# One layer on one core: the first tile's load shared by two queues, and the early order of ScalarE and VectorE changed

## What is computed

```
def step(carry, kv_t):                      # over the 128 tokens of a sequence
    p, q, o = carry
    no = max(o, u + kt); A = exp(o - no); E = exp(u + kt - no)
    y = (A * p + E * vt) / (A * q + E)
    no2 = max(w + o, kt); A2 = exp(w + o - no2); E2 = exp(kt - no2)
    return (A2 * p + E2 * vt, A2 * q + E2, no2), y

x = x + wkv(w, u, layernorm(x), ctx)
xf = layernorm(x)
gates = softmax(xf @ gate_w + gate_b); combine = the two largest, others 0
routed = sum over e of combine[:, e] * (gelu(xf @ ew1[e] + eb1[e]) @ ew2[e] + eb2[e])
shared = sum over s of gelu(xf @ sw1[s] + sb1[s]) @ sw2[s] + sb2[s]
x = x + shared + routed
```

## Time and profile before

| | us |
|---|---|
| median of three executions | 859.07 |
| lowest and highest of them | 858.18, 859.83 |
| the profiled execution | 859.92 |
| span of its instructions | 858.2 |
| TensorE busy in it | 835.7 |
| VectorE, ScalarE, GpSimd busy | 617.8, 467.1, 237.2 |

### The profile page before, as it was taken

The page is one execution under the profiler, slowest core; times in us unless marked ns, Lnnn a source line. Parts: engine busy times, 40 slices in busy tenths (PEclk is TensorE's granted clock), DMA queues, the critical chain, the costliest instruction groups (busy, mean ns, idle before and its releaser), DMA issues.

```text
span 858.2 us, 14380 instructions
## 1 busy us (share of the span) xinstructions
PE 835.7 (97%) x4102; PEld 692.2 (81%) x4102; DVE 617.8 (72%) x1244; ACT 467.1 (54%) x824; POOL 237.2 (28%) x277
## 2 busy tenths in 40 slices
PE   3899999999999999999999999999999999999998
PEld 2768888888888888878888888888888889998886
DVE  7987889976887778757787787576787544443694
ACT  6577776444466663534656464345555355656442
POOL 4110000233200000225000003232342488854870
PEclk9999999999999999999999999999999999999999
DMA  8913644389533333787433325867798388868987
GB/s 242 297 37 111 173 122 122 110 179 182 121 109 88 100 97 108 175 195 162 102 117 98 99 75 162 156 123 220 210 241 215 117 265 269 270 213 274 308 235 223
DMA packets 130144, 144.24 MB, mean 168 GB/s; under 512 B 11010, under 2 KB 89402, under 8 KB 129568
## 3 DMA queue, kind: packets, MB, share of 16 engines
q1 hardware_dynamic: 117792, 108.88, 48.3%
q0 software_dynamic: 11344, 33.50, 13.2%
q10 hardware_dynamic: 944, 1.07, 0.4%
HBM read 120.43 MB, written 22.98 MB: 167 GB/s over the span
## 4 chain that ended last, share of the span: by engine, by line
PE 89%; DMA 2%; SPq 1%; DVE 1%; issue 1%; ACT 0%; DVEq 0%; ACTq 0%
PE up L640 13%; PE up L642 12%; PE up L641 12%; PE acc L701 12%; PE acc L703 12%; PE acc L707 12%; PE up L885 5%; DMA w_raw<-in_L_ffn_sw 2%; PE acc L640 1%; PE acc L642 1%; PE acc L641 1%; PE misc L666 1%; PE up L666 1%; PE acc L811 1%; PE up L803 1%
## 5 line engine op out<-in xcount | busy, mean ns | idle before, releaser
L640 PE MATMUL up<-xs,w1hi 128*128 128x512 f32 (+1 forms) x512 | 198.4, 387 | 0.1
L642 PE MATMUL up<-xs,w1lo 128*128 128x512 f32 (+1 forms) x512 | 195.5, 382 | 0.0
L641 PE MATMUL up<-xs,w1hi 128*128 128x512 f32 (+1 forms) x512 | 195.4, 382 | 0.0
L963 ACT ACTIVATE hhi<-up,b_col 128x512 fp32r<-128x512 f32 x128 | 86.6, 676 | 199.2 <-PE up L642 161.1
L701 PE MATMUL acc<-w2hi,hhi 128*128 128x512 f32 x486 | 189.7, 390 | 0.0
L703 PE MATMUL acc<-w2lo,hhi 128*128 128x512 f32 x486 | 189.3, 389 | 0.0
L1239 DVE TENSOR_TENSOR hlo<-hf,hhi 128x512 fp32r<-128x512 f32 x128 | 85.6, 669 | 68.7 <-ACT hhi L963 28.6
L707 PE MATMUL acc<-w2hi,hlo 128*128 128x512 f32 x486 | 130.7, 389 | 0.0
L640 PEld LDWEIGHTS up<-xs,w1hi 128*128 128x128 f32 x512 | 96.2, 188 | 18.9 <-issue 0.7
L642 PEld LDWEIGHTS up<-xs,w1lo 128*128 128x128 f32 x512 | 96.2, 188 | 18.7
L641 PEld LDWEIGHTS up<-xs,w1hi 128*128 128x128 f32 x512 | 96.3, 188 | 17.9
(11 more groups left out here) (270 smaller groups left out, 1124.1 us busy)
## 6 DMA issues: line engine op xcount, KB each, us to landing
w_raw<-in_L_ffn_sw SPq DMA_DIRECT2D x256, 256.0 KB, 3.1
expert_rows<-ysb SPq DMA_DIRECT2D x47, 256.0 KB, 3.8
xn_rows<-kn POOLq DMA_DIRECT2D x16, 256.0 KB, 8.5
e2raw<-in_L_ffn_ew SPq DMA_DIRECT2D x16, 256.0 KB, 6.6
ew_sb<-in_L_ffn_ew SPq DMA_DIRECT2D x16, 256.0 KB, 6.8
X<-in_x SPq DMA_DIRECT2D x12, 256.0 KB, 8.6
vin<-in_ctx SPq DMA_DIRECT2D x12, 256.0 KB, 11.6
out<-X SPq DMA_DIRECT2D x12, 256.0 KB, 4.4
```

The costliest lines, as they stand in the source:

```text
L640: nc.tensor.matmul(o, lhs[0], rhs[0], start=start, stop=False)
L641: nc.tensor.matmul(o, lhs[0], rhs[1], start=False, stop=False)
L642: return nc.tensor.matmul(o, lhs[1], rhs[0], start=False, stop=stop)
L963: nc.scalar.activation(hhi[:, slot, tok], up[slot][:, tok], ACT.Gelu, bias=bias).then_inc(h_hi, 1)
```

## The change

Tile 0's four parts are issued two by SP and two by ScalarE's queue, the latter ahead of the vectors. VectorE normalizes tile 0 (`early_ln1_apply(0)`) ahead of `tables`. ScalarE makes `grow`, then tile 0's exponential, then `keep`, then copies tile 0's values, and then makes `boost`. VectorE does `ev` right after the first scan, ahead of `h`, for all four tiles (for tiles 2 and 3 behind `early_ln2_apply`); `ev` waits for the values itself, as `hv` did and does. The names of the counting semaphores follow the new order.

```diff
--- before.py
+++ after.py
@@ -340,11 +340,11 @@
         early2 = Steps(sem("early2"), "s a veps")
         tab = Steps(sem("tab"), "wu neg pos down uw cap")
         boost_arg = sem("boost_arg")
-        tabs0 = Steps(sem("tabs0"), "keep grow boost")
+        tabs0 = Steps(sem("tabs0"), "grow keep boost")
         rec0 = Steps(sem("rec0"), "ln rec")
         tabs = Steps(sem("tabs"), "grow relu boost keep")
         wt = Steps(sem("wt"), "tk tv")
-        wkv0 = Steps(sem("wkv0"), "es cq sq h hv den ev cp sp num nt nr y")
+        wkv0 = Steps(sem("wkv0"), "es cq sq ev h hv den cp sp num nt nr y")
         wkv = Steps(sem("wkv"), "es h ev hv cq sq den cp sp num nt nr y ty")
         wexp = Steps(sem("wexp"), "e ln rec")
         ln2 = Steps(sem("ln2"), "s0 s1 s2 s3 a0 a1 a2 a3 veps")
@@ -528,7 +528,8 @@
                              sw1_c[p // CPS, p % CPS]).then_inc(pw1_in[p], 16)
                 sp.dma_start(early_w2(p), sw2_c[p // CPS, p % CPS]).then_inc(pw2_in[p], 16)
 
-            load_tiles([0])
+            for g in (0, 1):
+                sp.dma_start(X2[32 * g:32 * g + 32, 0, 0], xq[0, g, :, 0]).then_inc(x_tile[0], 16)
             load_tiles([1])
             load_tiles([2, 3])
             load_values([2, 3])
@@ -1057,6 +1058,8 @@
                 nc.scalar.copy(e2hi[:, e], e2raw[:, e]).then_inc(r2hi, 1)
 
             nc.scalar.preload_act_table_set("natural_log_exp_and_others")
+            for g in (2, 3):
+                act.dma_start(X2[32 * g:32 * g + 32, 0, 0], xq[0, g, :, 0]).then_inc(x_tile[0], 16)
             for at, vector in ((0, decay), (CW, bonus)):
                 act.dma_start(wu[at + CB:at + CW], vector.rearrange("(b g p) -> b g p", g=GB, p=32)).then_inc(uw_in, 16)
                 act.dma_start(wu[at:at + CB], vector.rearrange("(b o p) -> b o p", o=1, p=32)
@@ -1083,11 +1086,11 @@
                 nc.scalar.activation(hf[:, n % RING, piece(n)], up[n % RING][:, up_piece(n)], ACT.Gelu,
                                      bias=b1_col[:, p:p + 1]).then_inc(pre_h, 1)
 
-            first_keep()
             first_grow()
             early_exp(0)
+            first_keep()
+            early_values(0)
             first_boost()
-            early_values(0)
             early_values(1)
             for b in range(CB // 2 - 1):
                 table_grow(b)
@@ -1361,6 +1364,7 @@
                                            in1=state(qq)[:, :, 0:TT], op0=ALU.min, op1=ALU.add))
 
             def early_ev(i):
+                dve.wait_ge(v_ok, i + 1)
                 edo(V.tensor_tensor(state(ev)[:, :, 1:], state(es)[:, :, 1:], values(i), ALU.mult))
 
             def early_num(i):
@@ -1642,15 +1646,15 @@
                 const(V.tensor_tensor(bias_s[:], bias_s[:], bias_g[:, 0], ALU.add))
 
             early_ln1(0)
+            early_ln1_apply(0)
             tables()
-            early_ln1_apply(0)
             early_ln1(1)
             early_es(0)
             early_scan(0)
+            early_ev(0)
             early_h(0)
             early_hv(0)
             early_den(0)
-            early_ev(0)
             early_num(0)
             early_result(0)
             early_ln1_apply(1)
@@ -1663,11 +1667,11 @@
             early_ln1_apply(2)
             early_es(1)
             early_scan(1)
+            early_ev(1)
             early_h(1)
             early_hv(1)
             early_den(1)
             early_ln1(3)
-            early_ev(1)
             early_num(1)
             early_ln1_apply(3)
             early_result(1)
@@ -1676,10 +1680,10 @@
             early_ln2(1)
             early_scan(2)
             early_ln2_apply(1)
+            early_ev(2)
             early_h(2)
             early_hv(2)
             early_den(2)
-            early_ev(2)
             early_num(2)
             early_result(2)
             early_es(3)
@@ -1687,10 +1691,10 @@
             early_ln2(2)
             early_scan(3)
             early_ln2_apply(2)
+            early_ev(3)
             early_h(3)
             early_hv(3)
             early_den(3)
-            early_ev(3)
             early_num(3)
             early_result(3)
             x_lo(2, 1, 2, x_bank[2])
```

## The result

The median of twenty executions is 861.5 us (860.51 to 867.91) against 859.3 us (858.18 to 862.82) for the kernel before in as many: a ratio of 1.0029, 95% interval 1.0015 to 1.0042. (The ratios in this document come from all executions of both kernels; they are not the quotients of the medians.) The change makes the kernel slower by 2.2 us. Forecast were 859.9 us, a range up to 861.2 and 0.14 for slower by over 0.2%.

A forecast was written before the change was run, and what follows sets the result against it. The start of TensorE's dense matmuls was taken to bound the kernel, with VectorE setting it. VectorE's path +0.06 and ScalarE's reciprocal path +0.8, the later counting, turned median 859.07 into 859.9 us, range 858.5 to 861.2.

The forecast's parts named there:

- slower by over 0.2%: Rival at TensorE's wait for tile 1's `vin`: parts land ever later, price 1.75 us, 860.8 and above; chance 0.14.
- What bounds the kernel: TensorE's dense matmuls, busy all 186.00 us from 64 to 250, carry any shift of their start to the end.
- First tile on two queues: Tile 0's load: statistics start at about 3.45 us, `kn` at 5.36, 0.83 earlier, keys' transposes done at 7.07.
- What ScalarE's queue pays: Two added parts free ScalarE's queue 0.75 to 0.95 us later; 0.8 taken, so at 7.31.
- Orders, tables and `ev`: ScalarE and VectorE lists: tables and `ev` order cost nothing; `es` starts at 9.23 us, 0.27 later.
- the sum: Tile 0's product: VectorE's path +0.06 us, ScalarE's path to the reciprocal +0.8; the later one counts.
- Values of tile 1: `vin` on ScalarE's queue: landing time kept at 4.9 us, so values shift by their issue, 0.8.
- The upper bound: Landing of tile 1's values: if the quarters' trend continues, 1.84 per microsecond of later issue, 0.95 gives 1.75 us.
- The page's figure: DMA landing of 64 KB estimated at 2.15 us; tile 1's values not late, sum +0.06 in place of +0.8.

The follow-up runs named there:

- e7: Kernel before, with tile 1's values issued by SP behind tile 1's rows and their copy behind the reciprocal; 859.35 us against 860.51, ratio 0.9991.
- e4: Changed kernel, with ScalarE's copy of tile 1's values moved behind tile 0's reciprocal; 861.69 us against 860.75, ratio 1.0010.
- e1: Changed kernel without its queue part: tile 0's four parts all on SP again, new orders kept; 863.64 us against 860.75, ratio 1.0030.
- e8: Kernel before, with two small constants (16 and 8 KB) at the head of ScalarE's queue, tile 0 all on SP; single execution 860.65 us beside 859.82.
- e8b: The same kernel as e8 run once more; single execution 860.09 us beside 859.82 for the kernel before.
- e5: Kernel before, with ScalarE's copy of tile 1's values moved behind tile 0's reciprocal; 859.24 us against 860.51, ratio 0.9997.
- e1b: The same kernel as e1 run once more; 860.4 us against 860.51 for the kernel before, ratio 1.0002.
- e3: Kernel before with tile 0 on two queues, plus two small constants issued by SP ahead of tile 1's rows; 862.02 us against 860.75, ratio 1.0026.
- e2: Kernel before with only the queue part, tile 0's four parts split between SP and ScalarE's queue; 862.51 us against 860.75, ratio 1.0039.
- e6: Changed kernel, with tile 1's values issued by SP behind tile 1's rows and their copy behind the reciprocal; 858.48 us against 860.51, ratio 0.9985.

## Why the prediction was wrong

**What bounds the kernel**: right. The front shift went through to the dense stream undiminished (+2.02 at the product and at 33.34, +2.03 at 64.22), and TensorE filled 185.89 of the 186.00 us from 64 to 250.

**First tile on two queues**: right. `kn` at 5.45 (forecast 5.36), the keys' transposes at 6.05 (5.95).

**What ScalarE's queue pays**: right in kind, a little short. Of 0.75 to 0.95 I took 0.8. The first vector took 0.58 us behind tile 0's parts too, so nothing was saved by its not being first, and the queue was free 0.95 later. ScalarE's dependence on its queue, read from 6.51 and 6.56, is shown by e7.

**Orders, tables and `ev`**: the order of events right, VectorE's own path too short. `es` was 0.49 later in place of 0.27. The values of tile 0, which I had at hand from 9.7, landed late as well and were copied only at 10.98, and `ev` waited for them a little (11.60 for 11.2). The path came out at +0.51 where the sum has +0.06; this stayed hidden behind the later reciprocal, and e4, which takes the reciprocal out of the way, shows it (16.51, +0.54). `boost` and `den` cost nothing. The +0.34 of the orders alone (e1) is another thing: there `kn` is not early, the tables behind it end `w_down` at 7.42, and `grow` waits for them until 7.45 with the queue free since 6.49.

**Values of tile 1**: this is the step that failed. "I take the landing time kept at 4.9, so the shift of the issue, 0.8". The landing time grew to 5.9, and the term was 2.02 in place of 0.8. The later issue alone would have left it nearly as I took it (5.2 and 5.3 in e8 and e8b). The upper bound, 1.75 from the slope of the eight quarters, was nearer, and even it fell short. I had named SP's transfers, moved up by 0.94, beside these and let them cost nothing in landing time; the runs give them about 0.84. The rest of the sum held, since the later of the two paths counts: 859.3 + 2.02 = 861.3, measured 861.5. The rival "slower by over 0.2%" was this mechanism with its place right, and its condition (transposes after 12.7) was met at 12.99; its chance of 0.14 was too low, as was the range's top.

**The page's figure.** The Trainium skill ("DMA: Bandwidth & Descriptors", section "Anatomy of one DMA — SWDGE (gpsimd) path") gives 2.0 us plus the bytes at 436 GB/s for DMAs that GpSimd issues, an estimated 2.15 us for 64 KB. The loads here are issued by SP and ScalarE, to which the forecast carried the figure over. The eight parts landed in 2.1 to 4.9 us before and in 2.9 to 5.9 after: only the first one, before the change, fits. In the Trainium skill the same page's section "Issuing engines are not separate DMA queues" says that issuing from several engines saves only the time of the issue. That fits what tile 0 gained (0.70 us for two issues less, 0.94 of issue time), and says nothing of what the queue that takes them over loses.

## What to carry to other kernels

A DMA issued from a compute engine's list delays that engine's next instruction by its issue time, here 0.47 us each; look where the queue's last issue ends and whether the first computation starts right there. When a load is moved between queues, price what lands later on both sides: here the two issues came out at the landing as 1.14 us, and the queue that became shorter sent its own loads sooner, which held up the others' by another 0.84. And ask which list entry waits for each load: a copy that nobody needs for ten microseconds, placed ahead of a reciprocal that is needed now, made the load critical.

## What the runs showed of the hardware

Equal 64 KB loads of one queue, issued one after another over 3.4 us, took ever longer to land: from 2.1 to 4.9 us in the kernel before and from 2.9 to 5.9 after. What was issued ahead in the same queue mattered by its number and hardly by its bytes (start of the transposes 12.28 with 24 KB ahead, 12.36 with 128 KB).

One execution can lose several microseconds in the dense stream, where TensorE otherwise has next to no gap. The profiled execution of e5 began that stream 0.28 us earlier than before and yet had a span of 861.8: the cast of a weight came late, because ScalarE waited for its DMA, and TensorE waited 3.3 us for the cast.

```profile
PE acc L701 <- ACT w2hi L946: 3.3, 1, 3.3
```

```profile
ACT w2hi L946 <- DMA w_raw<-in_L_ffn_sw: 23.4, 5, 11.7
```

The kernel before itself ran from 858.15 to 869.79 us over all its executions. Medians of twelve executions differed by 3 us for one and the same kernel (e1 863.64, e1b 860.4). The start of the dense stream repeated much better in three pairs of equal kernels (e1 64.56 and 64.50, e3 65.60 and 65.61, e8 65.51 and 65.55), and by 0.58 us in the fourth (e2 66.05 and 66.63). So a single trace tells a shift of over 0.6 us here and a repeated one a smaller shift, where medians of a dozen executions do not. The 0.28 of e5 and the 0.4 of e6 and e7 rest on single traces, the latter on two kernels that agree.
